# Self-attention of a decoder layer: where the causal mask is added, and the order of one block's steps on five engines

## What is computed

```
x = layernorm(x + self_attention(x))        # 16 heads of 32, rotary q and k, causal mask
x = layernorm(x + gamma * cross(x, ctx))    # 8 heads
x = layernorm(x + ffn(x))                   # 512 -> 2048 -> 512, quantised
```

```
q, k, v = x @ Wq.T, x @ Wk.T, x @ Wv.T ; q, k = rope(q), rope(k)
scores = q @ k.T / sqrt(32) ; scores = where(causal, scores, -inf)
out = softmax(scores) @ v ; return out @ Wo.T
```

## Time and profile before

| | |
|---|---|
| median of 3 executions | 1829.21 us (1828.71 to 1835.35) |
| profiled execution, its own time | 1833.27 us |
| its span, first to last instruction | 1831.5 us |
| PE busy over the span | 1609.7 us, 88% |
| DVE busy | 1546.8 us, 84% |
| ACT busy | 1377.0 us, 75% |
| POOL busy | 961.4 us, 52% |
| mean granted TensorE clock | 0.935 of full |

### The profile page before, as it was taken

How to read it: one execution, slowest core, us unless ns; L and a number is a source line. 1 busy time by engine, 2 the same in 40 slices (tenths; PEclk the granted TensorE clock), 3 DMA queues, 4 the chain that set the end, 5 groups by cost and what they waited for, 6 DMA issues and landing times.

```text
span 1831.5 us, 35203 instructions
## 1 busy us (share of the span) xinstructions
PE 1609.7 (88%) x11936; PEld 873.5 (48%) x12000; DVE 1546.8 (84%) x2086; ACT 1377.0 (75%) x2853; POOL 961.4 (52%) x1408
## 2 busy tenths in 40 slices
PE   6999999999998889999999999999777777767774
PEld 4777777777775333333333333333233333333331
DVE  5788888888887989999989899999489999899985
ACT  4666645555453578888888888888699999899994
POOL 6667667676674533355544555323445555545542
PEclk9999999999999799999999999999878888888886
DMA  3465443434337454444464654444333333333311
GB/s 136 147 183 175 127 120 112 136 105 130 115 117 189 109 105 112 108 118 120 108 175 131 168 120 118 108 118 104 118 98 104 104 105 104 104 104 104 104 47 35
DMA packets 119269, 217.10 MB, mean 119 GB/s; under 512 B 32241, under 2 KB 34705, under 8 KB 116785
## 3 DMA queue, kind: packets, MB, share of 16 engines
q1 hardware_dynamic: 110770, 213.64, 41.5%
q0 software_dynamic: 8320, 1.21, 0.4%
HBM read 137.67 MB, written 76.02 MB: 117 GB/s over the span
## 4 chain that ended last, share of the span: by engine, by line
PE 58%; issue 12%; DVE 10%; ACT 7%; DMA 6%; POOL 5%; SPq 1%; POOLq 0%; DVEq 0%; ACTq 0%
PE sums L1059 13%; PE bank L1076 12%; PE bank L549 11%; PE wide L1029 6%; PE sums L549 5%; DMA out<-c_result 3%; PE wide L599 3%; DVE stage L1710 2%; ACT stage L1595 2%; PE wide L591 2%; ACT b_prob L945 2%; DVE a_prob L469 2%; PE sums L611 2%; DMA b_xs<-b_max_part 2%; PE wide L586 1%
## 5 line engine op out<-in xcount | busy, mean ns | idle before, releaser
L969 DVE TENSOR_REDUCE b_smax<-wide 128x2 f32<-128x1024 f32 x512 | 620.5, 1225 | 60.4 <-PE wide L1029 48.6
L945 ACT ACTIVATE b_prob<-bank 128x512 f32<-128x512 f32 x1024 | 556.3, 599 | 111.6 <-PE bank L1076 101.1
L1076 PE MATMUL bank<-b_xs,b_cs 50*128 50x512 f32 x1024 | 329.5, 478 | 23.6 <-ACT b_prob L945 13.2
L1059 PE MATMUL sums<-b_prob,b_vT 128*32 128x256 f32 (+1 forms) x3584 | 318.8, 428 | 5.2 <-ACT b_prob L945 0.5
L1029 PE MATMUL wide<-b_cs,b_xs 48*128 48x512 f32 x1024 | 282.8, 436 | 9.1 <-DVE b_smax L969 7.6
L1888 PE MATMUL sums<-c_w,c_hqT 128*128 128x512 bf16 x481 | 170.2, 530 | 114.1 <-issue 106.8
L1076 PEld LDWEIGHTS bank<-b_xs,b_cs 50*128 50x128 f32 x1024 | 133.4, 187 | 234.4 <-ACT b_prob L945 172.6
L885 POOL TENSOR_SCALAR b_max_part<-b_neg_max 16x128 fp32r<-16x128 f32 x64 | 18.6, 291 | 322.6 <-ACT b_neg_max L936 322.5
L370 ACT ACTIVATE a_prob<-wide,a_neg_max 128x128 f32<-128x128 f32 x512 | 181.8, 417 | 3.9 <-DVE a_neg_max L461 3.9
L1888 PEld LDWEIGHTS sums<-c_w,c_hqT 128*128 128x128 bf16 x512 | 63.4, 128 | 210.8 <-issue 185.9
L895 POOL DMA_DIRECT2D b_xs<-b_max_part x256 | 134.2, 530 | 42.1 <-POOL b_max_part L888 37.3
(11 more groups left out here) (147 smaller groups left out, 3247.7 us busy)
## 6 DMA issues: line engine op xcount, KB each, us to landing
scratch_c_part<-a_c_part SPq DMA_DIRECT2D x64, 256.0 KB
scratch_x_part<-a_x_part SPq DMA_DIRECT2D x64, 256.0 KB
b_xs<-scratch_x_part SPq DMA_DIRECT2D x128, 128.0 KB, 3.1
b_cs<-scratch_c_part SPq DMA_DIRECT2D x128, 128.0 KB, 3.1
scratch_heads<-b_heads SPq DMA_DIRECT2D x64, 256.0 KB, 2.6
a_xT<-in_xT SPq DMA_DIRECT2D x32, 256.0 KB, 6.4
a_c_in<-in_ctx SPq DMA_DIRECT2D x32, 256.0 KB, 2.6
a_x<-in_x SPq DMA_DIRECT2D x32, 256.0 KB, 4.1
```

Source lines behind the costliest of these rows:

```text
L945: act.activation(prob[k % 8][:, :], e_ps[bank_of(k)][:, :], ACT.Exp, scale=0.25).then_inc(exp_done, 1)
L969: dve.tensor_reduce(smax[g][:, :, j, qc], m_ps[u % 2][:, :, :], AX.X, ALU.max, negate=True).then_inc(max_done, 1)
L1059: last = pe.matmul(av_ps[2 * XD * h:2 * XD * (h + 1), cols], vT[p][:, lc, XG * g + h, :], prob[(XG * n + 2 * j + e) % 8][:, cols], start=( ...
L1076: pe.matmul(e_ps[bank_of(2 * u + e)][:, :], cs[p][g][half(e), j, lc * P:(lc + 1) * P], xs[p][g][half(e), j, :], start=True, stop=True).the ...
```

## The change

- The mask is no longer written by PE. ACT makes a tile `barred` once (the mask times -1, so 1e30 where a position may not be seen). q is scaled by the negative of the old factor, so that `scores` leaves negated scores in the banks, with `start=True` for each product and no mask product.
- `maxima` becomes four instructions for each bank, one for each head: a `tensor_tensor_reduce` that adds `barred` to the negated scores, writes the sum to `prob` in SBUF and gives the minimum of the row as accumulator output. `exponentials` then reads `prob` (with scale -1) in place of the bank.
- All four copies of transposed probabilities are ACT's; DVE has none.
- PE's step has another order: `project(t, 2)`, which is v, moves behind the transposes of k and of bank 1, and the output projection is cut into three thirds of four products, put between the later transposes.
- DVE's `out_low` moves ahead of the last two divisions.
- POOL's step has another order after `rope_q`, and `split_x1` is of block t - 5; the store of `x_part` is of block t - 6 and stands first in SP's step. At the end of the stage POOL's `begin(1)` stands behind one more step.

The core of the diff (left out are semaphore declarations, the load of one mask in place of four copies, and loop ends):

```diff
@@ -92,7 +92,8 @@
     wo_lo = sb("wo_lo", [P, KC, D], F32R)
     ident = sb("ident", [P, P])
     ident_b = sb("ident_b", [P, P], BF16)
-    mask4 = sb("mask4", [P, HPC, P], BF16)
+    mask = sb("mask", [P, P], BF16)
+    barred = sb("barred", [P, P])
     cos = sb("cos", [P, DH])
     sin = sb("sin", [P, DH])
     xT = sb("xT", [P, D])
...
@@ -184,6 +185,13 @@
             sp.dma_start(stage[n][:, :, :], t_in[w]).then_inc(w_ld[n], 16)
 
         def step(t, on):
+            if on(6):
+                b = t - 6
+                sp.wait_ge(x1_split, 2 * b + 2)
+                for j in range(PARTS):
+                    dst = scratch["x_part"][bass.ds(b * PARTS * P + j * P, P), :]
+                    sp.dma_start(dst.rearrange("(d h) q -> h d q", h=XH), x1_part[:, j, :].bitcast(F32)).then_inc(
+                        part_st, 16)
             if on(0):
                 if later(t):
                     sp.wait_ge(xT_split, t)
...
@@ -193,13 +201,6 @@
                 if later(b):
                     sp.wait_ge(c_split, 2 * b)
                 sp.dma_start(c_in[:, :], rows(t_in["ctx"], b)).then_inc(c_ld, 16)
-            if on(5):
-                b = t - 5
-                sp.wait_ge(x1_split, 2 * b + 2)
-                for j in range(PARTS):
-                    dst = scratch["x_part"][bass.ds(b * PARTS * P + j * P, P), :]
-                    sp.dma_start(dst.rearrange("(d h) q -> h d q", h=XH), x1_part[:, j, :].bitcast(F32)).then_inc(
-                        part_st, 16)
             if on(2):
                 b = t - 2
                 if later(b):
...
@@ -309,14 +309,14 @@
         def step(t, on):
             if on(1):
                 rope_q(t - 1)
+            if on(5):
+                split_x1(t - 5)
+            if on(0):
+                split_xT(t)
+            if on(3):
+                power(t - 3)
             if on(2):
                 split_ctx(t - 2)
-            if on(0):
-                split_xT(t)
-            if on(4):
-                split_x1(t - 4)
-            if on(3):
-                power(t - 3)
 
         pool.wait_ge(pool_const, 1)
         pool.wait_ge(const_ld, 16 * CONSTS)
...
@@ -324,10 +324,13 @@
             step(t, lambda k: 0 <= t - k < NB)
         begin(0)
         step(NB + 2, lambda k: k > 2)
+        step(NB + 3, lambda k: k > 3)
         begin(1)
-        step(NB + 3, lambda k: k > 3)
+        step(NB + 4, lambda k: k > 4)
 
     def scalar(act):
+        act.wait_ge(const_ld, 16 * CONSTS)
+        act.activation(barred[:, :], mask[:, :], ACT.Copy, scale=-1.0).then_inc(barred_done, 1)
         for n in range(4):
             act.wait_ge(w_ld[n], 16)
             dst = w_hi[:, :, n * D:(n + 1) * D] if n < 3 else wo_hi[:, :, :]
...
@@ -339,7 +342,7 @@
             if later(b):
                 act.wait_ge(q_rope, 4 * b)
             act.activation(q_raw[:, :], q_ps[:, :], ACT.Copy,
-                           scale=float(1.0 / np.sqrt(np.float32(DH)))).then_inc(q_raw_done, 1)
+                           scale=float(-1.0 / np.sqrt(np.float32(DH)))).then_inc(q_raw_done, 1)
 
         def values(b):
             act.wait_ge(v_proj, b + 1)
...
@@ -364,10 +367,8 @@
         def exponentials(b, j):
 
             act.wait_ge(max_done, 4 * b + j + 1)
-            if later(b):
-                act.wait_ge(prob_tr, 4 * b - 3 + j)
             for c in range(KC):
-                last = act.activation(prob[:, j, c, :], s_ps[j][:, c * P:(c + 1) * P], ACT.Exp,
+                last = act.activation(prob[:, j, c, :], prob[:, j, c, :], ACT.Exp, scale=-1.0,
                                       bias=neg_max[:, j, c:c + 1], accum_out=den[:, j, c:c + 1])
             last.then_inc(exp_done, 1)
 
...
@@ -402,8 +403,12 @@
             if on(1):
                 prob_transposed(t - 1, 0)
                 prob_transposed(t - 1, 1)
+            if on(1):
+                prob_transposed(t - 1, 2)
             if on(0):
                 q_transposed(t)
+            if on(1):
+                prob_transposed(t - 1, 3)
 
         def sum_ffn(t):
             if 3 <= t < 2 * KC + 3:
...
@@ -457,9 +463,12 @@
 
             dve.wait_ge(score_done[j], b + 1)
             if later(b):
-                dve.wait_ge(exp_done, 4 * b - 3 + j)
-            dve.tensor_reduce(neg_max[:, j, :], s_ps[j][:, :].rearrange("p (c n) -> p c n", c=KC), AX.X, ALU.max,
-                              negate=True).then_inc(max_done, 1)
+                dve.wait_ge(prob_tr, 4 * b - 3 + j)
+            for c in range(KC):
+
+                last = dve.tensor_tensor_reduce(prob[:, j, c, :], s_ps[j][:, c * P:(c + 1) * P], barred[:, :], 1.0,
+                                                -MASKED, ALU.add, ALU.min, neg_max[:, j, c:c + 1])
+            last.then_inc(max_done, 1)
 
         def normalise(b, j):
 
...
@@ -492,13 +501,6 @@
                 dve.wait_ge(x1_split, 2 * b)
             dve.tensor_scalar(x1[:, :], x1_sum[:, :], mv[:, 0:1], rstd[:, 0:1], ALU.subtract,
                               ALU.mult).then_inc(x1_done, 1)
-
-        def prob_transposed(b, j):
-            dve.wait_ge(prob_tr, 4 * b + j + 1)
-            if later(b):
-                dve.wait_ge(av_done, b)
-            dve.tensor_copy(probT[:, j, :, :], s_ps[j][:, :].rearrange("p (c n) -> p c n", c=KC)).then_inc(
-                pT_dve, 1)
 
         def step(t, on):
             if on(1):
...
@@ -509,17 +511,13 @@
                 normalise(t - 1, 1)
             if on(0):
                 rope_k(t)
+            if on(2):
+                out_low(t - 2)
             if on(1):
                 normalise(t - 1, 2)
                 normalise(t - 1, 3)
-            if on(2):
-                out_low(t - 2)
-            if on(1):
-                prob_transposed(t - 1, 2)
             if on(3):
                 norm_x1(t - 3)
-            if on(1):
-                prob_transposed(t - 1, 3)
             if on(2):
                 residual(t - 2)
                 statistics(t - 2)
...
@@ -580,16 +578,12 @@
             pe.wait_ge(qT_done, b + 1)
             pe.wait_ge(kT_done, b + 1)
             if later(b):
-                pe.wait_ge(pT_act, 2 * b)
-                pe.wait_ge(pT_dve, 2 * b)
-            for j in range(HPC):
-                pe.matmul(s_ps[j][:, :], ident_b[:, :], mask4[:, :, :].rearrange("p j n -> p (j n)"),
-                          start=True, stop=False)
+                pe.wait_ge(pT_act, 4 * b)
             for c in range(KC):
                 for j in range(HPC):
                     r = slice(DH * j, DH * (j + 1))
                     mm = pe.matmul(s_ps[j][:, c * P:(c + 1) * P], qT[r, c, :], kT[r, c, :],
-                                   start=False, stop=(c == KC - 1))
+                                   start=True, stop=True)
                     if c == KC - 1:
                         mm.then_inc(score_done[j], 1)
 
...
@@ -602,8 +596,7 @@
         def attend(b):
 
             pe.wait_ge(v_done, b + 1)
-            pe.wait_ge(pT_act, 2 * b + 2)
-            pe.wait_ge(pT_dve, 2 * b + 2)
+            pe.wait_ge(pT_act, 4 * b + 4)
             if later(b):
                 pe.wait_ge(sum_done, b)
             for c in range(KC):
...
@@ -612,31 +605,47 @@
                                      probT[:, j, c, :], start=True, stop=True)
             last.then_inc(av_done, 1)
 
+        def out_third(b, n):
+            if n == 0:
+                pe.wait_ge(oT_hi_done, b + 1)
+                if not later(b):
+                    pe.wait_ge(w_lo_done, 4)
+                pe.wait_ge(oT_lo_done, b + 1)
+            a, w = ((oT_hi, wo_hi), (oT_hi, wo_lo), (oT_lo, wo_hi))[n]
+            for c in range(KC):
+                last = pe.matmul(o_ps[:, :], a[:, c, :], w[:, c, :], start=(n == 0 and c == 0),
+                                 stop=(n == 2 and c == KC - 1))
+            if n == 2:
+                last.then_inc(out_done, 1)
+
         def out_projection(b):
-            pe.wait_ge(oT_hi_done, b + 1)
-            pe.wait_ge(oT_lo_done, b + 1)
-            if not later(b):
-                pe.wait_ge(w_lo_done, 4)
-            triple(o_ps[:, :], oT_hi, oT_lo, wo_hi, wo_lo).then_inc(out_done, 1)
+            for n in range(3):
+                out_third(b, n)
 
         def step(t, on):
             if on(0):
                 project(t, 0)
                 project(t, 1)
-                project(t, 2)
             if on(1):
                 transpose_prob(t - 1, 0)
             if on(0):
                 transpose_k(t)
             if on(1):
                 transpose_prob(t - 1, 1)
+            if on(0):
+                project(t, 2)
+            if on(2):
+                out_third(t - 2, 0)
+            if on(1):
                 transpose_prob(t - 1, 2)
             if on(0):
                 transpose_q(t)
+            if on(2):
+                out_third(t - 2, 1)
             if on(1):
                 transpose_prob(t - 1, 3)
             if on(2):
-                out_projection(t - 2)
```

(2 more changed lines are left out.)

10 lines of the change are left out of this document (5 added, 5 removed).

## The result

The changed kernel takes 1961.99 us (median of 4 executions, 1955.14 to 1965.34) against 1829.18 for the kernel before beside it: a ratio of 1.0713, with a 95% interval from 1.0676 to 1.075. The forecast was 1961.0. The number is right, but by luck: two terms of its sum and one item that it costed at nothing are not, and the errors cancel. The rest of this text is about that.

What follows compares the result with a forecast made beforehand. PE was taken to bound the kernel before. 30 steps of 3.5 plus 0.7 us (126) and 6 at the stage's end, added to 1833.3, gave 1965 profiled, 1961 for the median; range 1885 to 2010.

Steps and rivals of the forecast that it cites:

- What bounds the kernel before: First stage: PE, busy 98.40 of 100 us, sets the step of 17.69 us, with about 0.5 us of slack.
- The exposed rotation: DVE's rotation of k, no longer covered by PE's projection of v, adds 2.8 us to the step's loop.
- I take 0.34: 16 x 0.34 = 5.4 us: DVE's maxima: 16 pairs of addition with minimum and read-out, 5.4 us (4.3 to 7.7) against 2.48 before.
- the lower bound of 0.27: Least time in us for one DVE pair, from a straight line through wider instructions, taken at 128 columns.
- I take 2.7: DVE's two divisions behind the maxima, one or both slowed beside POOL: 2.7 us (1.75 to 3.4).
- The sum of 21.2: Step in us between output projection ends: 2.0 + 5.4 + 2.7 + 2.8 + 8.3, against 17.69, plus 3.5.
- rival B: DVE's pair costs 0.27, POOL is missed, the clock stays up: 18.5 us a step, 1859 us; chance 0.12.
- The clock, 1.05 in two steps of three: PE's stop of 4.0 us halves its clock for 3.4 us, losing 1.05 us, counted as 0.7 a step.
- SP's store moved to the front of its step: SP's store of x_part waits for an earlier step's split and delays loads only by its issue; costed at nothing.
- POOL's new order: POOL's power waits for DVE's statistics, context split and q rotation behind; q's input comes later anyway; costed at nothing.
- Plus 6: End of first stage: one more turn of split, store and landing before b_max_part, 6 us (0 to 8).
- All the added time is a plain wait of PE for `a_k_rot`: PE idle before the transpose of k in some 30 places, 3.5 to 4.5 us each.

Runs made afterwards that it cites:

- v_first: The changed kernel with one edit: PE projects v right behind k again, ahead of the transposes of k; 1946.05 us, ratio 1.0579 to the kernel before.
- store_early_fill: store_early plus eight extra, useless products on PE just ahead of the transposes of k; 1864.53 us, ratio 1.0126 to the kernel before.
- store_early: The changed kernel with SP's store of x_part for block t-5, between the loads of x transposed and the context; 1896.94 us, ratio 1.0321.

## Why the prediction came out right

Point by point, in its own order:

- **What bounds the kernel before:** right in part. PE is nearly full, but the circle of POOL and the store, 17.4 to 18.05 us, is as long as the step, and the prediction did not look for it.
- **The exposed rotation:** right. PE waits before `a_k_rot` wherever v's projection stands behind it, and v_first removes that wait.
- **"I take 0.34: 16 x 0.34 = 5.4 us":** wrong. A pair costs 0.21 us, below the lower bound of 0.27 and below the 0.3 that it had named as a sign against itself; 16 are 3.4. The bound was a straight line through rows of 256 and 512 columns, and the read-out was taken as additional. Here an addition shown as 0.29 long is followed by the next one after 0.21, with the read-out beside that one.
- **"I take 2.7" for the two divisions:** 1.7 (311.17 to 312.88). POOL met only the end of the second. The long division of the earlier trace rows ended 0.55 us after POOL's subtraction (259.59 and 259.04), not 0.69.
- **The sum of 21.2:** wrong by these two, by 0.3 in the rotation (2.5 for 2.8) and 0.4 in PE's part (7.9 for 8.3), and in its form. DVE is done with divisions 2.0 + 3.4 + 1.7 = 7.1 us after the output projection, PE with k's projection 7.9 after. So the circle goes through PE and the rotation only: 7.9 + 2.5 + 7.9 = 18.3. The prediction had this under rival B as "the floor", with 18.5 and, for the kernel, 1859 us, which is 1.016 of its 1829; store_early_fill, where neither the store nor the clock disturbs it, has 18.37 and a ratio of 1.0126. B's "no fall of the clock" at a stop of about 2 us did not hold: in store_early it fell after stops of 2.15.
- **The clock, 1.05 in two steps of three:** right in place; a fall costs 1.6 us in store_early, where it shows in the time and comes in two steps of three. In the changed kernel it comes in most steps (21 stretches in some 24 steps from 100 to 600 us) and is mostly covered. The Trainium skill, page "TensorE: Matmul & The Clock Gate", section on HAM oscillation, has it in each turn. The waits in its example are of about 3 to 5 us, longer than the 2.15 to 2.3 us here, so the steps of 18.34 beside those of 19.93 neither bear it out nor refute it.
- **At nothing: "SP's store moved to the front of its step, which waits for a split made a step ago, and delays the loads behind it by no more than its issue":** this is the step that failed. It asked what the store delays and not what delays the store. In front of its step it is behind the last wait of the step before, for the split of the context, and behind the five starts that follow that wait. What it stores was ready at 304.9, it started at 313.05, it had landed for POOL at 323.05, and POOL, DVE and PE waited in turn: a circle of 20.15 us. "POOL's new order", also at nothing, was costed with its input in time; it put the split of the context behind `power`, and so behind DVE's statistics, one of the links of the circle. Moving the store alone takes 0.039 off the ratio (store_early), some 72 us.
- **"Plus 6" at the end:** 29.8. One more turn did come ahead of `b_max_part`, as forecast, and cost 8.8. The two turns before it became longer by 18.6, by the same circle with the second stage's loads in it, and that had been left out.
- **The start, "a microsecond or so once" for ACT's wait:** 3.4 (first scores at 31.5 against 28.1). It is not ACT's wait: the kernels that keep that wait and project v first have them at 27.9 to 28.7, the others at 31.5 to 33.1. It belongs to PE's order.
- **"All the added time is a plain wait of PE for `a_k_rot`":** false; 2.3 us a step are that, and removing it alone gives back 25 of 133 us. The other sign that it had named against itself, DVE waiting before it rotates k, came too (0.63).

The sum came out by luck: the steps were to add 126 us and add 94.5, mostly for another reason, while the end adds 29.8 in place of 6 and the start 3.4: 132 forecast, 129.5 measured between the profiled executions. Two circles of nearly the same length, 18.3 or 19.9 through k and 20.2 or more through the store, run beside each other in the changed kernel; either alone makes it slower than the kernel before (store_early 1.032, v_first 1.058), and together they cost little more than the longer one.

What stays open: why a store that starts at 313.05 has landed only near 323. It stands behind five others started in the 2.6 us before it, SP takes 2.71 us to start it, and the DMA engines are busy (a share of 0.82 to 0.89 from 314 to 316); at the end of the stage, where its start takes 1.20, POOL's next split comes 5.4 and 6.3 us after it (692.93 to 698.34, 713.28 to 719.57). How these parts share the 10 us was not tried. Nor was POOL's old order tried with the changed SP, and the single long steps of the changed kernel (up to 27.0) are not explained one by one.

## What to carry to other kernels

A queue that only starts transfers is an engine like the others: when an item on it is moved, ask what is the last wait ahead of the item in its new place, also when that wait belongs to the step before, and follow from there until the way ends or comes back to where it began. Where it comes back, its whole length is a lower bound of the step, whatever the busy times say. And when two such circles are about equally long, undoing one alone shows only a part of its worth. Here v's place gives 25 us with the late store and 98 with the early one, and the store's place 72 us with v late and 146 with v first.

## What was not expected of the hardware

- DVE's addition with minimum over 128x128 shows 288 ns, but 16 of them with their read-outs take 0.21 us each, start to start, with the read-out (0.08) beside the next one.
- ACT's exponential of 128x128 from SBUF takes 0.385 us to the next one with its read-out (309.15 to 309.54 in the timeline, 16 in a row alike), where the one from PSUM takes 0.34.
- Starting the same two transfers of `a_x_part` takes SP 2.71 us right behind five others (313.05), and 1.19 when it had started nothing for 5 us. But it takes 1.20 right behind thirteen others at the stage's end (692.93), so the number ahead does not decide it alone; what does is not shown.
- Eight useless products, 2.08 us of PE's time, in each step, made the program 32 us shorter; the clock stayed at 1.00 with them.
